# Loading the types of 26 slots into registers at once, in a graph transformer layer

## The reference

```python
def _typed_matmul(x, W, node_type):
    all_t = jnp.einsum('ni,tio->tno', x, W)
    return all_t[node_type, jnp.arange(x.shape[0])]
k = _typed_matmul(h, k_linears, node_type).reshape(n, N_HEADS, D_K)
q = _typed_matmul(h, q_linears, node_type).reshape(n, N_HEADS, D_K)
v = _typed_matmul(h, v_linears, node_type).reshape(n, N_HEADS, D_K)
q_att = jnp.einsum('nhd,rhde->rnhe', q, relation_att)
v_msg = jnp.einsum('nhd,rhde->rnhe', v, relation_msg)
```

## Time and profile before

| | |
|---|---|
| median of 3 runs | 2135.72 us (2134.32 to 2140.13) |
| profiled execution | 2138.12 us, its span 2136.9 us |
| mean granted TensorE clock | 0.962 of full speed |
| busy: TensorE matmul, weight load | 89%, 67% of the span |
| busy: VectorE, ScalarE, GpSimd | 77%, 68%, 56% of the span |
| chain that ended last | PE 61%, DVE 16%, issue 7%, ACT 5%, DMA 4%, POOL 4%, DVEq 2% |
| tables' stage | some 122 to 525 us; lines L797, L804, L818, L1762, L1275 |

### The profile page before, as it was taken

The page is one execution under the profiler, slowest core; times in us unless marked ns, Lnnn a source line. Parts: engine busy times, 40 slices in busy tenths (PEclk is TensorE's granted clock), DMA queues, the critical chain, the costliest instruction groups (busy, mean ns, idle before and its releaser), DMA issues.

```text
span 2136.9 us, 37589 instructions
## 1 busy us (share of the span) xinstructions
PE 1894.5 (89%) x10412; PEld 1437.7 (67%) x10412; DVE 1655.1 (77%) x4094; ACT 1460.7 (68%) x4926; POOL 1198.8 (56%) x1218
## 2 busy tenths in 40 slices
PE   6999998998789999999999998999999973947999
PEld 5865555554577887777778777777777752635666
DVE  8857776655489999989999998998999975876511
ACT  7855555555368888888888887888888873733321
POOL 0033333432777777767777776776777741602565
PEclk9999999999799999999999999999999986967999
DMA  7958789899899999999999999999999926671321
GB/s 236 316 190 324 314 324 299 339 360 385 290 329 304 307 326 310 311 299 305 314 302 317 322 324 298 299 313 286 314 318 317 318 75 198 183 258 48 123 83 51
DMA packets 271463, 583.73 MB, mean 273 GB/s; under 512 B 45078, under 2 KB 185962, under 8 KB 264600
## 3 DMA queue, kind: packets, MB, share of 16 engines
q0 software_dynamic: 93936, 384.51, 51.8%
q1 hardware_dynamic: 177320, 196.82, 28.3%
HBM read 407.81 MB, written 176.99 MB: 274 GB/s over the span
## 4 chain that ended last, share of the span: by engine, by line
PE 61%; DVE 16%; issue 7%; ACT 5%; DMA 4%; POOL 4%; DVEq 2%; SPq 0%; POOLq 0%; ACTq 0%
PE bank L999 11%; PE bank L983 8%; PE bank L818 7%; PE bank L1191 4%; PE bank L797 4%; PE bank L1178 4%; PE bank L879 4%; POOL arena L2477 3%; PE bank L964 3%; ACT arena L1393 3%; PE bank L664 3%; DMA arena<-table,arena 2%; PE bank L1143 2%; PE bank L708 2%; PE bank L720 2%
## 5 line engine op out<-in xcount | busy, mean ns | idle before, releaser
L2477 POOL DMA_INDIRECT arena<-table,arena x880 | 866.1, 984 | 327.0 <-issue 252.0
L1393 ACT ACTIVATE arena<-arena 128x64 f32<-128x64 f32 x3432 | 839.7, 340 | 0.0
L999 PE MATMUL bank<-arena 128*128 128x260 f32 x1760 | 436.8, 391 | 42.7 <-DVE arena L2103 39.7
L999 PEld LDWEIGHTS bank<-arena 128*128 128x128 f32 x1760 | 322.5, 191 | 115.8 <-issue 69.7
L2017 DVE TENSOR_TENSOR arena<-bank,arena 128x512 f32<-128x512 f32 x440 | 300.8, 686 | 88.6 <-PE bank L983 58.0
L983 PE MATMUL bank<-arena 128*128 128x256 bf16 x2640 | 336.7, 276 | 6.9 <-DVE arena L2017 6.9
L983 PEld LDWEIGHTS bank<-arena 128*128 128x128 bf16 x2640 | 259.0, 99 | 63.6 <-DVE arena L2017 8.0
L2027 DVE TENSOR_REDUCE arena<-arena 128x16 f32<-128x1024 f32 x220 | 266.1, 1209 | 0.4 <-issue 0.2
L818 PE MATMUL bank<-arena 64*128 64x512 f32 x832 | 207.2, 613 | 16.1 <-DVE arena L1762 10.8
L1275 ACT COPY arena<-bank 128x512 f32<-128x512 f32 x260 | 148.9, 595 | 82.4 <-PE bank L818 82.0
L2103 DVE TENSOR_TENSOR arena<-arena,bank 128x260 f32 x440 | 184.3, 419 | 11.6 <-PE bank L999 6.7
(11 more groups left out here) (329 smaller groups left out, 3020.9 us busy)
## 6 DMA issues: line engine op xcount, KB each, us to landing
arena<-q_parts SPq DMA_DIRECT2D x440, 192.0 KB
arena<-chunk_rel SPq DMA_DIRECT2D x220, 128.0 KB, 5.5
arena<-table,arena POOLq DMA_INDIRECT x880, 5.2
node_rows<-arena SPq DMA_DIRECT2D x24, 512.0 KB, 6.4
xl_and_sum<-arena SPq DMA_DIRECT2D x3, 3072.0 KB, 11.5
arena<-in_x SPq DMA_DIRECT2D x12, 512.0 KB, 7.6
xn<-arena SPq DMA_DIRECT2D x12, 512.0 KB, 7.8
xT<-arena SPq DMA_DIRECT2D x12, 512.0 KB, 7.9
```

Of the source, the lines that this page charges most:

```text
L999: ins = TE.matmul(bank[b][:, 0:AW], lhsT=so[p % 2][:, c % 2, j, :], rhs=values_of(c, j), start=j == 0, stop=j == HALF - 1)
L1393: ins = A.activation(seg, seg, ACT.Copy, scale=rows[:, C + h:C + h + 1])
L2477: G.indirect_dma_start(rows_of_pair(p, i % 2 * HALF + j), None, d_tab_rows[0:N * R, :], bass.IndirectOffsetOnAxis(ap=idxE[:, g, j, c:c + 1 ...
```

## The change

The number of types that one load brings goes from 8 to 26, in both places. The calls are then at slots 0 and 26, with 26 values each, in place of 0, 8, 16, 24, 32, 40 and 48. The registers are picked by s % 26. The other loads of the kernel stay as they are.

```diff
-PLACES = 8
+PLACES, TYPES_AT_ONCE = 8, 26
...
-            if s % 8 == 0:
+            if s % TYPES_AT_ONCE == 0:
                 _, w_at = nc.values_load_multi_w_load_instructions(
-                    w_off_i[0:1, s:min(NTS, s + 8)], engines=[PEENG], min_val=0, max_val=(T - 1) * KQV,
+                    w_off_i[0:1, s:min(NTS, s + TYPES_AT_ONCE)], engines=[PEENG], min_val=0, max_val=(T - 1) * KQV,
                     skip_runtime_bounds_check_because="a type is below T")
...
-                ins = TE.matmul(bank[b][:, 0:C], lhsT=xgT[s % 2][:, c, :], rhs=W[c][:, KV:][:, bass.ds(w_at[s % 8], C)],
+                ins = TE.matmul(bank[b][:, 0:C], lhsT=xgT[s % 2][:, c, :], rhs=W[c][:, KV:][:, bass.ds(w_at[s % TYPES_AT_ONCE], C)],
                                 start=c == 0, stop=c == CC - 1)
...
         def kv_weights_of(s):
 
             nonlocal w_at
-            if s % 8 == 0:
+            if s % TYPES_AT_ONCE == 0:
                 _, w_at = nc.values_load_multi_w_load_instructions(
-                    w_off_i[0:1, s:min(NTS, s + 8)], engines=[DVEENG], min_val=0, max_val=(T - 1) * KQV,
+                    w_off_i[0:1, s:min(NTS, s + TYPES_AT_ONCE)], engines=[DVEENG], min_val=0, max_val=(T - 1) * KQV,
                     skip_runtime_bounds_check_because="a type is below T")
...
             for c in range(CC):
-                ins = V.tensor_copy(Wkv[s % 2][:, c, :], W[c][:, bass.ds(w_at[s % 8], KV)])
+                ins = V.tensor_copy(Wkv[s % 2][:, c, :], W[c][:, bass.ds(w_at[s % TYPES_AT_ONCE], KV)])
```

## The result

The changed kernel takes 2145.08 us (median of 17 runs), the kernel before 2138.64 in as many runs beside it: 1.0033 times as long, 95% interval 1.0024 to 1.0042. Forecast were 2136.3 us, from 2124 to 2147, and no difference that can be told. The time lies within the range, near its upper end. Of the 8.8 us by which it exceeds the forecast, 2.9 are the base's: the forecast started from a median of three runs, 2135.72. The rest is the change's: it costs 6.4 us where +0.6 was forecast. The loss lies about at the bound of 0.3% that the prediction set, so the forecast of no difference (0.67, against 0.18 for slower) is just missed, or just met within the interval. The profiled execution has a span of 2143.4 us, against 2136.9: +6.5.

What follows compares the result with a forecast made beforehand. TensorE was taken to bound the tables' stage. Added 3.9 + 6.5 + 3.7 + 2.5 = 16.6 us against 16.0 removed gave +0.6 us on a median of 2135.7: 2136.3 us, range 2124 to 2147.

Steps and rivals of the forecast that it cites:

- What bounds the stage, and which gaps are the loads': Tables' stage: TensorE sets the pace; its gaps at slots 8 to 48 that belong to loads sum to 19.7 us.
- What the change removes: Loads at slots 8, 16, 24, 32, 40, 48 go; slot 26 keeps one boundary of 3.7: 16.0 us gone.
- a microsecond in which TensorE idles is a microsecond of the span: Tables' stage: it goes at TensorE's pace, busy 359.0 of 391.5 us, so each idle microsecond lengthens the span.
- (a): Slot 0: both engines load at once, 18 more values each, bare but for 0.1 us of cover: +3.9 us.
- (b): VectorE's load for slot 26: 18 more values at 0.36 us each, all paid by TensorE: +6.5 us.
- (c): TensorE's load for slot 26: 18 more values at 0.21 us each, no overlap with (b): +3.7 us.
- (d): Clock at slot 26: after the idle of (b) and (c), TensorE works at half clock: +2.5 us, ends 0 and 5.0.
- A: All loads: a load costs the same for any number of values; 16.0 us gained, 2119.7 us; chance 0.10.
- B: Slots 0 and 26: values cost 0.22 us each on both engines, clock holds; -4.0 us, 2131.7; chance 0.22.
- C: Slots 0 and 26: 0.46 us a value on VectorE, 0.37 on TensorE, clock falls; +8.7 us, 2144.4; chance 0.18.
- D: Load calls: 26 values need several instructions, or live registers cost moves; about +2 us, 2138; chance 0.04.

Runs made afterwards that it cites:

- The runs with the late store: SyncE's store of the chunk offsets moved behind the edge marks: 1.0032 in the kernel before (loads of 8), 1.0021 in the changed kernel (26), both against the kernel before.
- the kernel with the loads ahead: Against the kernel before, all 52 types loaded ahead of the stage and kept in 52 registers: 0.9937, measured again 0.9934 (2126.2 us).

## Why the prediction was right or wrong

*What bounds the stage, and which gaps are the loads'*: right. The gaps at slots 8, 16, 24, 40 and 48 went with the loads and came back as steps of the ladder (3.5, 4.1, 3.5, 3.1, 1.2; rows 3 gave 3.7 on the average and 1.2).

*What the change removes*: wrong by 3.8 us, the largest miss. The prediction counted 4.2 us for slot 32 and got 0.5. The step that failed was "a microsecond in which TensorE idles is a microsecond of the span". It doesn't hold at slot 32, because TensorE has to wait for a gather there in any case, which the store of the chunk offsets holds up. The kernel before idles 2.56 and 1.68 us for its loads and then 3.2 us in two waits at L664. The changed kernel has no load there, comes to L664 sooner and waits 5.0 us (4.71 and 0.33), 1.9 more; and behind the long wait it works at half clock, 5.83 us for sixteen L818 in place of 4.10 and 0.69 for two L664 in place of 0.44, 2.0 more. 4.2 - 1.9 - 2.0 leaves 0.3. The profile before had the sign of it: 49 GB/s at a DMA share of 0.87. I read the DMA share over the whole stage and not the GB/s slot by slot. The runs with the late store show the cause, though by themselves they give back 2.6 us and not 4.2. On small elements the Trainium skill has a rule, on the page "DMA: Bandwidth & Descriptors", section "Specifications": below 512 bytes the DMA engine reads, modifies and writes. These rows agree with slow small elements; the mechanism itself no run here shows.

*(a) Slot 0*: +3.9 forecast, and the gap is 3.67. The step that was missing is the clock, which I had only at slot 26: 3.2 us of work at 0.50 here, +1.6. Measured 5.4.

*(b) VectorE at slot 26*: the gap forecast at 1.8 + 6.5 = 8.3 is 9.68. Each of the 18 values more cost 0.43 us ((11540 - 3711) / 18 ns) where I took 0.36. My reason for less, that the transfers thin out once TensorE stops, came too late to matter: the share is still 0.94 up to 318 us, 1.5 us before the load's end.

*(c) TensorE at slot 26*: the load forecast at 6.7 us took 6.4, the gap 3.37 and not 5.5, since the eight matmuls ahead ran at half clock and covered more of it. The value was right and its reason wrong: 0.2 us is no property of TensorE's loads but goes with the quiet behind VectorE's stall: without that stall the same load takes 12.0 us.

*(d) The clock at slot 26*: 2.5 forecast; 3.79 - 1.99 = 1.8 behind the first gap and 1.7 behind the second, 3.5. With (b) and (c), 9.68 + 3.37 + 3.5, the slot comes to 16.6 us by its gaps and clock, and to 16.0 by the ladder, where 16.4 were forecast.

Together: 5.4 + 16.0 - 15.9 = +5.5 us for the stage, where the forecast had 3.9 + 16.4 - 19.7 = +0.6. Of the 4.9 us between them 3.8 are slot 32, 1.5 slot 0, and -0.4 slot 26. That slot 26 comes out so near is partly luck: its gaps were forecast at 13.8 us and are 13.05, its clock at 2.5 and is 3.5, in part since the eight matmuls between the gaps ran slow and covered the second load.

*The rivals*: A (flat price) is refuted by every load of 26. B (quiet price everywhere) holds for slot 0 and for TensorE, 6.0 to 6.4 us; there the Trainium skill's page "Runtime: NRT & Kernel Launch", with about 200 ns a register in "Instruction fetch mechanics", is near: (6034 - 2067) / 18 = 220 ns. The page speaks of loads from HBM, and these come from SBUF. It doesn't hold for VectorE within the stage, at 435. C named the measured time almost exactly (2144.4), but on a base that is 2.9 us too low: its difference was +8.7 us, and +6.4 were measured. Two of its three parts came true, VectorE's price and the clock behind both slots; the third, 0.37 on TensorE, didn't, and the lost return of slot 32 came in its place. So the match of its time is chance. D: there was one TENSOR_LOAD of 26 values to a call.

## What to carry to other kernels

A load of registers stalls its engine longer the more values it brings, so fewer and longer loads don't save the stall; in this kernel they made it worse, since a long one outlasts the work that TensorE has queued. Put the loads where the engine waits anyway or has matmuls queued, and keep the values in registers: that alone was faster here (0.9934). If two engines must load within such a stage, let both do it at the same place: with one engine's loads drawn apart from the other's, the stage was 12.6 and 22.8 us longer than before, with both together 5.6. And before counting a removed gap as gained, look whether TensorE would wait there for something else; a low GB/s in that very stretch is the sign, whatever the DMA share says.

## What the runs showed of the hardware

- One TENSOR_LOAD takes 26 values, and 28 in the kernel with the loads ahead. With no transfers beside it, it took 6.0 us on VectorE and 6.3 on TensorE (2.07 and 2.10 for eight), 0.22 to 0.23 us for each value more. In the tables' stage it took 9.9 to 12.0 us, at DMA shares of 0.63 to 0.77 (247 to 298 GB/s), but 6.4 there where the transfers had run dry (0.09). Transfers alone don't explain it: in the edges' stage VectorE's loads of eight took 1.83 us beside 297 GB/s, half of the 3.7 in the tables' stage. That difference stays open.
- While a store of 1024 elements of 2 bytes was under way, the core's DMA traffic was 49 GB/s for 10 us (38 in the changed kernel), 324 before it and 388 behind it. Moved ten slots on, the same store took 26.5 to 54.5 us in place of 17 to 21.
- Gaps of TensorE of 3.67 us (slot 0), 4.71 (slot 33) and 9.68 (slot 26) were each followed by a granted clock of 0.50. So was the one of 3.37, but the clock had been 0.50 ahead of it too. No line between gaps that cost clock and gaps that don't can be drawn from these rows: behind gaps of 1.8 to 2.6 us the clock held in the kernel before, and in the kernel with 26 values on TensorE alone it was 0.60 behind one of 2.37 us.
